# ScalarE, not SyncE, issues half of the weight loads at a change of layer: eight sequences through six layers on one core

## The chip, the cores and the metric

The kernel runs on one core of a Trainium2 chip. The metric is the time of one execution in microseconds (us) on the device. Of three runs of the kernel before, the median is 1677.21 us (1673.2 to 1680.72).

## The reference, cut to what matters

The input `x` is 8 sequences of 256 tokens with 128 channels, in float32. A first attention layer (16 heads of 8) is added to `x`. Then 6 layers follow, each with a windowed attention and a feed-forward part:

```python
for i in range(DEPTH):            # DEPTH = 6
    x = attn_layer(shift_tokens(x), Wqkv[i], q_scale[i], k_scale[i], Wo[i]) + x
    x = ffn_layer(shift_tokens(x), ln_g[i], ln_b[i], W1[i], b1[i], W2[i], b2[i]) + x

def attn_layer(x, Wqkv, qs, ksc, Wo):       # 16 heads of 64, window 32
    q, k, v = split(x @ Wqkv)
    q, k = l2norm(q) * qs, l2norm(k) * ksc  # then a rotary embedding of both
    ...                                     # softmax over this window and the one before
    return out @ Wo
```

## The kernel before, in words

A setup block computes the first attention layer and brings the weights of all six layers into a form of eight *banks* per layer in the device's memory (`weights`, 512 KB a bank): banks 0 and 1 give q, 2 and 3 give k, and 4 to 7 give the product of the value weights with the output projection, `u`. The rest is one pipeline over 48 *units* (`UNITS`), unit n being sequence n % 8 in layer n // 8. Only one layer's banks are resident, in the tile `w_t`.

A step of the pipeline is written out by hand for each engine (the functions `step`), and it mixes stages of up to four units: `after` (the next), `u`, `before` and `last`. The Python loop unrolls all steps, so each engine runs a fixed list of instructions, and semaphores alone tie the engines together. All waits of an instruction are `wait_ge` just ahead of it.

- **TensorE** multiplies the input of a unit, split in a high and a low part, with the banks: `proj(u, t, j)` (L1893, L1898, L1902) for token tile t and bank j, into two banks of PSUM in turn. At the first unit of a layer the first `proj` of each bank waits for that bank's load (`w_in[j]`). It transposes q and k (`transpose_qk`, L1917), makes the scores (`scores`, L1931 and L1939), transposes the probabilities (L1949), multiplies them with `vk` (`values`, L1961) and does the feed-forward part (L1982 to L2031). The banks 0 to 3 of the next unit are used at the end of a step: `proj(after, 0, 0)` to `proj(after, 0, 3)`. For the last unit of a layer their last readers are `proj(u, 1, 0)` to `proj(u, 1, 3)`, in the first half of the same step.
- **ScalarE** squares the q and k products (`square`, L1638), copies transposed q and k into `qT` and `kT` (L1660, L1664), copies `u` into the tile `un` (L1648), copies the transposed probabilities (L1681) and the output `o` (L1691), and computes exponentials and GELU. At the last unit of a layer (`split_layer`) it also makes the high part of the next W1 (`w_hi`, L1763), between `feed_hi` and `copy_qkT(u, 0, 1, 0)`. It issues no DMA.
- **VectorE** makes the sums of the squares, the rotary products and the softmax steps; **GpSimd** the norms and the second half of the rotary embedding.
- **SyncE** issues every DMA. `copy_v(n, t)` rearranges `un` into `vk` by 14 or 16 DMAs (L1255), once `u` of unit n is complete and the values of the unit before are read. `renew(layer, j)` waits until the last unit of the old layer has read bank j and issues the load of 512 KB (`load_weights`, L222). SyncE works through its list in order: between layers it is `copy_v` of unit 6 of the layer, then `renew` of banks 4, 5, 0, 1, 2, 3, 6, 7, then `copy_v` of unit 7.

The semaphore `qk_p` counts the products of banks 0 to 3, eight a unit: `qk_p.at(n, 4 + j)` is reached when token tile 1 has read bank j. `square(u, 1, kind, half)` waits for the same count for j = 2 * kind + half.

Of the kernel before, what the change touches and what calls it, by code (L numbers as in the profile page):

```python
# [33 lines left out]
B = 8  # L34
# [25 lines left out]
UNITS = L * B  # L60
BANKS = 8
QK_BANKS = 4
# [26 lines left out]
def build(nc, x, w_heads, bq_heads, bk_heads, w_v, b_v_rows, w_proj, b_proj_rows, wqk, q_scale_rows, k_scale_rows, wvt, wo,  # L89
          feed_cols, w1, w2, rope, ident, win_mask, win_pick, causal, positions, slope_heads, one_row, weights, out):  # L90
    with ExitStack() as ctx:
# [52 lines left out]
        qk_p = signal("qk_p", 8)  # L144
# [75 lines left out]
        def load_weights(sp, at, j):  # L220
            src = weights[bass.ds(at, 1), :, :].rearrange("o p n -> p (o n)")
            sp.dma_start(w_t[:, j, :, :].rearrange("p k n -> p (k n)").bitcast(F32), src).then_inc(w_in[j].sem, 16)  # L222
# [992 lines left out]
        def index(u):  # L1215

            return u[0] * 2 + u[1]
# [9 lines left out]
        def live(u):  # L1227

            n = index(u)
            return not isinstance(n, int) or 0 <= n < UNITS  # L1230
# [7 lines left out]
        with nc.Block() as block:  # L1238
            @block.sync
            def _(sp):  # L1240
                def copy_v(n, t):


                    value = un_a[t].at(n, 3)
                    sp.wait_ge(av_p.sem, value)
                    sp.wait_ge(un_a[t].sem, value)
                    for w in range(4 * t, 4 * t + 4):
                        for back in (1, 0):
                            if w - back < 0:
                                continue  # L1250
                            tile, k = (w - back) // 4, (w - back) % 4
                            for hp in range(2):
                                lo = 64 * hp + 32 * (1 - back)
                                src = un[32 * k:32 * k + 32, (n % 2) * TT + tile, hp, :]
                                sp.dma_start(vk[lo:lo + 32, w, :, :].rearrange("p a c -> p (a c)"),  # L1255
                                             src).then_inc(vk_in[t].sem, 16)

                def renew(layer, j):
                    qk = j < QK_BANKS
                    at = layer * BANKS + j  # L1260
                    read = qk_p.at(layer * B - 1, QK_BANKS + j) if qk else u_p[0].at(layer * B - 1, j - QK_BANKS)
                    for used in (qk_p,) if qk else u_p:
                        sp.wait_ge(used.sem, read)
                    load_weights(sp, at, j)

                def load_w1(layer):
                    sp.wait_ge(w1l_g.sem, w1l_g.at(layer - 1))
                    sp.dma_start(w1_s[:, :], w1[bass.ds(layer, 1), :, :].rearrange("o p n -> p (o n)")).then_inc(w1_in.sem, 16)

                def load_w2(layer):  # L1270
                    last = w2_p.at(layer * B - 1)
                    sp.wait_ge(w2_p.sem, last)
                    sp.dma_start(w2_s[:, :, :], w2[bass.ds(layer, 1), :, :, :].rearrange("o p k n -> p (o k) n")).then_inc(w2_in.sem, 16)


                sp.wait_ge(zeroed.sem, 1)
                for n in range(2):
                    for t in range(TT):
                        copy_v(n, t)
                for i in range(2):  # L1280
                    sp.wait_ge(qk_stored[i].sem, qk_stored[i].at(L * QK_BANKS // 2 - 1, 15))
                for half in range(2):
                    sp.wait_ge(u_stored[half].sem, u_stored[half].at(L - 1, 15))
                for layer in range(L - 1):
                    for i in range(2, 7):
                        for t in range(TT):
                            copy_v(layer * B + i, t)
                        if i == 4:
                            load_w1(layer + 1)
                    renew(layer + 1, 4)  # L1290
                    renew(layer + 1, 5)
                    renew(layer + 1, 0)
                    renew(layer + 1, 1)
                    renew(layer + 1, 2)
                    renew(layer + 1, 3)
                    renew(layer + 1, 6)
                    renew(layer + 1, 7)
                    copy_v(layer * B + 7, 0)
                    copy_v(layer * B + 7, 1)
                    copy_v(layer * B + 8, 0)  # L1300
                    copy_v(layer * B + 8, 1)
                    copy_v(layer * B + 9, 0)
                    load_w2(layer + 1)
                    copy_v(layer * B + 9, 1)
                for i in range(2, B):
                    for t in range(TT):
                        copy_v(i + (L - 1) * B, t)

                sp.wait_ge(sc_p.sem, sc_p.at(UNITS - 1, 1))
                sp.wait_ge(spilled.sem, 16 * B)  # L1310
                sp.dma_start(x1_again, out.rearrange("b (t p) c -> p (b t) c", p=P)).then_inc(x1_in.sem, 16)
                sp.wait_ge(x1_in.sem, 16)
                for b in range(B):
                    sp.wait_ge(res_d.sem, res_d.at(b))
                    sp.dma_start(out[b, :, :].rearrange("(t p) c -> p t c", p=P), x1_again[:, b * TT:(b + 1) * TT, :]).then_inc(out_done.sem, 16)
                sp.wait_ge(out_done.sem, 16 * B)
# [307 lines left out]
            def _(act):  # L1624
# [6 lines left out]
                def square(u, t, kind, half):  # L1631
# [4 lines left out]
                    if t > 0 or not (isinstance(n, int) and n < 1):  # L1636
                        act.wait_ge(ss_d.sem, ss_d.before(n, 2 * t + kind - 1))
                    S.activation(sq[:, kind, half * 512:(half + 1) * 512], ps[:, PJ + PJ_BANK[t][2 * kind + half], :],  # L1638
                                 ACT.Square).then_inc(sq_a.sem, 1)

                def copy_u(u, t, j):
                    if not live(u):
                        return
                    n = index(u)
                    act.wait_ge(u_p[t].sem, u_p[t].at(n, j))
                    if not (isinstance(n, int) and n < 2):
                        act.wait_ge(vk_in[1].sem, vk_in[1].at(n - 2, vk_in[1].per - 1))
                    S.activation(un[:, (u[1] % 2) * TT + t, j // 2, (j % 2) * HALF:(j % 2 + 1) * HALF],  # L1648
                                 ps[:, PJ + PJ_BANK[t][QK_BANKS + j], :], ACT.Copy).then_inc(un_a[t].sem, 1)
# [131 lines left out]
                def step(m, s):  # L1781
                    after, u, before, last = ((m, s + k) for k in (1, 0, -1, -2))
                    square(u, 0, 0, 1)
                    copy_qkT(before, 1, 0, 1)
                    shift_hi(after)
                    copy_pT(last, 1)
                    square(u, 0, 1, 0)
                    copy_qkT(before, 1, 1, 0)
                    square(u, 0, 1, 1)
                    exps(before, 0)  # L1790
                    root_seed(u, 0)
                    copy_o(last, 1)
                    if index(last) == UNITS - 1:
                        finish_copy(0)
                        finish_copy(1)
                    copy_qkT(before, 1, 1, 1)
                    copy_u(u, 0, 0)
                    residual_hi(last)
                    copy_u(u, 0, 1)
                    copy_u(u, 0, 2)  # L1800
                    copy_u(u, 1, 0)
                    copy_center(last)
                    square_x(last)
                    if index(last) == UNITS - 1:
                        finish_copy(2)
                        finish_copy(3)
                    copy_u(u, 1, 1)
                    square(u, 1, 0, 0)
                    copy_qkT(u, 0, 0, 0)
                    square(u, 1, 0, 1)  # L1810
                    copy_qkT(u, 0, 0, 1)
                    copy_pT(before, 0)
                    square(u, 1, 1, 0)
                    square(u, 1, 1, 1)
                    if index(last) == UNITS - 1:
                        finish_copy(4)
                        finish_copy(5)
                    feed_scale(last)
                    if index(last) == UNITS - 1:
                        finish_copy(6)  # L1820
                    feed_cols(before)
                    feed_hi(last)
                    copy_qkT(u, 0, 1, 0)
                    exps(before, 1)
                    root_seed(u, 1)
                    copy_qkT(u, 0, 1, 1)
                    copy_o(before, 0)
                    gelu(last, 0)
                    copy_u(u, 1, 2)
                    copy_u(u, 1, 3)  # L1830
                    gelu(last, 1)
                    copy_u(u, 0, 3)
                    copy_qkT(u, 1, 0, 0)
                    square(after, 0, 0, 0)
                    gelu(last, 2)
# [375 lines left out]
```

## Time and profile before

| | us |
|---|---|
| median of three runs | 1677.21 |
| the profiled execution, its time | 1680.03 |
| the profiled execution, its span | 1678.2 |
| TensorE, matmuls busy | 1620.7 (97%) |
| VectorE busy | 1478.2 (88%) |
| GpSimd busy | 1331.9 (79%) |
| ScalarE busy | 1328.8 (79%) |
| mean granted clock of TensorE | 0.992 of full |

The times of single instructions come from the profiled execution. PE stands for TensorE's matmuls, PEld for its weight loads, DVE for VectorE, ACT for ScalarE, POOL for GpSimd, SPq for SyncE's queue of DMA issues. The duration of an issue is the time of the issuing queue, not that of the transfer; the time to landing counts from the start of the issue until the data are there. A name such as `w_t<-weights_dram` is output<-input. The brackets at the end of a row of a timeline give the idle time of the engine ahead of the instruction and what ended it; "issue" stands there where the profile shows no releaser.

### The profile page before, as it was taken

To read this page: it belongs to the slowest core of one execution; us is meant where nothing else is said; L and a number is where in the kernel's file an instruction comes from. 1 tells how busy PE (TensorE), PEld (TensorE's weight loads), DVE (VectorE), ACT (ScalarE), POOL (GpSimd) and SP (SyncE) were. 2 spreads that over 40 slices of the span, in tenths; PEclk is the share of its full clock that TensorE was granted. 3 is DMA by queue.
4 is the path that set the end of the run, shared out by engine and by line. 5 is a ranking of instruction groups with operands and counts; after the bars stand their busy time and mean duration, and the time that the engine had idled before them with its cause. 6 is when DMAs were issued, how large, how long until landed. Compare 5 with 4: busy or idle time off the path is not lost.

```text
span 1678.2 us, 70646 instructions
## 1 busy us (share of the span) xinstructions
PE 1620.7 (97%) x29222; PEld 1410.5 (84%) x29222; DVE 1478.2 (88%) x2314; ACT 1328.8 (79%) x2789; POOL 1331.9 (79%) x1798
## 2 busy tenths in 40 slices
PE   7999869999999999999999999999999999999997
PEld 5777647888889889898988989898898988889886
DVE  6887749999899999899999999999999998999984
ACT  6888746878778788888878888787888887888874
POOL 7777568888788888888888788888888888888870
PEclk9999989999999999999999999999999999999999
DMA  3588517565865656857566765658566667656654
GB/s 125 176 295 323 199 26 162 119 147 133 231 146 128 155 128 155 228 128 164 119 159 167 194 146 134 149 128 244 124 154 137 143 150 207 156 128 148 139 131 111
DMA packets 101407, 265.78 MB, mean 158 GB/s; under 512 B 26720, under 2 KB 34912, under 8 KB 101088
## 3 DMA queue, kind: packets, MB, share of 16 engines
q1 hardware_dynamic: 101088, 261.26, 61.6%
q8 instruction: 232, 3.80, 1.0%
q14 instruction: 87, 0.71, 0.1%
HBM read 45.15 MB, written 27.26 MB: 43 GB/s over the span
## 4 chain that ended last, share of the span: by engine, by line
PE 74%; POOL 4%; SPq 3%; issue 2%; ACT 2%; DVE 1%; DMA 1%; POOLq 0%; ACTq 0%; DVEq 0%
PE ps L1893 17%; PE ps L1902 13%; PE ps L1961 9%; PE ps L1917 9%; PE ps L1939 7%; PE ps L1949 4%; PE ps L2031 3%; SPq L1255 3%; PE ps L2018 2%; PE ps L2020 2%; PE ps L2019 2%; PE ps L1931 2%; POOL rot L1339 1%; POOL rot L1397 1%; PE ps L1992 1%
## 5 line engine op out<-in xcount | busy, mean ns | idle before, releaser
L1339 POOL TENSOR_TENSOR rot<-rot 128x512 f32<-128x512 f32 x380 | 491.6, 1309 | 45.6 <-DVE rot L1474 45.6
L1474 DVE TENSOR_TENSOR rot<-ps,rope_l 128x1024 f32<-128x1024 f32 x380 | 462.8, 1219 | 27.4 <-ACT sq L1638 15.0
L1397 POOL TENSOR_TENSOR rot<-rot,rnorm 128x1024 f32<-128x1024 f32 x190 | 361.9, 1905 | 17.7 <-POOL rnorm L1367 0.4
L1648 ACT ACTIVATE un<-ps 128x512 f32<-128x512 f32 x384 | 229.6, 598 | 102.3 <-PE ps L1893 41.7
L1893 PE MATMUL ps<-w_t,xs_hi 128*128 128x512 f32 x880 | 298.0, 419 | 5.6 <-issue 3.8
L1902 PE MATMUL ps<-w_t,xs_hi 128*128 128x256 f32 x1284 | 262.9, 297 | 14.9 <-PEq L374 11.1
L1638 ACT ACTIVATE sq<-ps 128x512 f32<-128x512 f32 x380 | 227.8, 599 | 51.7 <-PE ps L1893 29.1
L1460 DVE TENSOR_REDUCE ssum<-sq 128x16 f32<-128x1024 f32 x190 | 229.9, 1210 | 13.7 <-ACT sq L1638 13.7
L1917 PE MATMUL ps<-ident_s,rot 128*128 128x128 f32 x1536 | 234.3, 275 | 6.0 <-ACT kT L1664 4.1
L1902 PEld LDWEIGHTS ps<-w_t,xs_hi 128*128 128x128 f32 x1284 | 196.3, 190 | 25.3 <-issue 20.4
L1917 PEld LDWEIGHTS ps<-ident_s,rot 128*128 128x128 f32 x1536 | 179.5, 140 | 40.9 <-issue 20.6
L1961 PE MATMUL ps<-vk,pT 128*32 128x128 f32 (+1 forms) x6624 | 189.6, 267 | 0.6 <-ACT pT L1681 0.6
L1902 PE MATMUL ps<-w_t,xs_lo 128*128 128x256 f32 x642 | 180.4, 281 | 0.0
L1961 PEld LDWEIGHTS ps<-vk,pT 128*32 128x32 f32 x6624 | 163.8, 110 | 16.6 <-issue 15.7
L1893 PEld LDWEIGHTS ps<-w_t,xs_hi 128*128 128x128 f32 x880 | 138.4, 189 | 35.3 <-ACT un L1648 8.4
L1893 PE MATMUL ps<-w_t,xs_lo 128*128 128x512 f32 x389 | 154.4, 397 | 0.0
L1939 PEld LDWEIGHTS ps<-kT,qT 64*32 64x32 f32 x12288 | 146.0, 105 | 7.6 <-issue 1.3
L1939 PE MATMUL ps<-kT,qT 64*32 64x64 f32 x12288 | 149.3, 225 | 0.4 <-issue 0.2
L1902 PEld LDWEIGHTS ps<-w_t,xs_lo 128*128 128x128 f32 x642 | 121.3, 189 | 0.0
L1518 DVE TENSOR_TENSOR prob<-ps,linv 128x1024 f32<-128x1024 f32 x96 | 117.6, 1225 | 3.1
L1485 DVE TENSOR_REDUCE smax<-ps 128x16 f32<-128x1024 f32 x96 | 116.5, 1213 | 3.1 <-PE ps L1939 3.1
L1502 DVE TENSOR_REDUCE lsum<-ps 128x16 f32<-128x1024 f32 x96 | 116.6, 1215 | 2.7 <-ACT ps L1672 2.7
(158 smaller groups left out, 3565.1 us busy)
## 6 DMA issues: line engine op xcount, KB each, us to landing
vk<-un SPq DMA_DIRECT2D x1440, 128.0 KB
w_t<-weights_dram SPq DMA_DIRECT2D x48, 512.0 KB, 6.9
weights_dram<-rot SPq DMA_DIRECT2D x12, 1024.0 KB, 5.1
weights_dram<-sq SPq DMA_DIRECT2D x24, 512.0 KB, 3.7
raw<-wqk_dram SPq DMA_DIRECT2D x24, 256.0 KB, 4.2
wvt_s<-wvt_dram SPq DMA_DIRECT2D x12, 256.0 KB, 5.3
wo_s<-wo_dram SPq DMA_DIRECT2D x12, 256.0 KB, 6.4
w_s<-w_dram SPq DMA_DIRECT2D x6, 341.0 KB, 4.3
```

The costliest lines, as they stand in the source:

```text
L1339: last = G.tensor_tensor(cos[:, :, s, :], cos[:, :, s, :], sin[:, :, 1 - s, :], ALU.add)
L1397: G.tensor_tensor(v, v, rnorm[:, t, kind * H:(kind + 1) * H, None].broadcast_to([P, H, D]), ALU.mult).then_inc(nrm_g.sem, 1)
L1460: V.tensor_reduce(ssum[:, t, kind * H:(kind + 1) * H], sq[:, kind, :].rearrange("p (h e) -> p h e", h=H), AX_X, ALU.add).then_inc(ss_d.sem, 1)
L1474: V.tensor_tensor(dst, src[:, None, :, :].broadcast_to([P, 2, H // 2, D]), tab[:, :, None, :].broadcast_to([P, 2, H // 2, D]), ALU.mult).t ...
L1518: V.tensor_tensor(pairs, tile_scores(t).rearrange("p (hp a) k -> p hp a k", hp=2), inv, ALU.mult).then_inc(pn_d.sem, 1)
L1638: S.activation(sq[:, kind, half * 512:(half + 1) * 512], ps[:, PJ + PJ_BANK[t][2 * kind + half], :], ACT.Square).then_inc(sq_a.sem, 1)
L1648: S.activation(un[:, (u[1] % 2) * TT + t, j // 2, (j % 2) * HALF:(j % 2 + 1) * HALF], ps[:, PJ + PJ_BANK[t][QK_BANKS + j], :], ACT.Copy).t ...
L1893: last = M.matmul(bank, v, w_t[:, j, w, :], start=i == 0, stop=i == 2)
L1902: last = M.matmul(bank[:, cols], v, w_t[:, j, w, cols], start=i == 0, stop=i == 2)
L1917: last = M.transpose(ps[:, TP, a * P:(a + 1) * P], rot[:, kind, 0, c * P:(c + 1) * P], ident_s[:, :])
L1939: last = M.matmul(out_s, qT[rows, par, a, 32 * w:32 * w + 32], kT[rows, a, 32 * w:32 * w + 64], start=False, stop=a == PAIRS - 1)
L1961: last = M.matmul(ps[32 * k:32 * k + 32, SO[t], cols], pT[:, a, 32 * k:32 * k + 32], vk[:, 4 * t + k, a, cols], start=a == 0, stop=a == PA ...
```

## The change

ScalarE gets a function `renew_qk`, which issues the load of one of banks 0 to 3 in the step of a layer's last unit, each behind the square of the same bank's product of token tile 1. SyncE keeps banks 4, 5, 6 and 7 in their order.

```diff
                     renew(layer + 1, 4)
                     renew(layer + 1, 5)
-                    renew(layer + 1, 0)
-                    renew(layer + 1, 1)
-                    renew(layer + 1, 2)
-                    renew(layer + 1, 3)
                     renew(layer + 1, 6)
                     renew(layer + 1, 7)
...
+                def renew_qk(u, j):
+                    if not live(u) or index(u) % B != B - 1 or index(u) == UNITS - 1:
+                        return
+                    n = index(u)
+                    act.wait_ge(qk_p.sem, qk_p.at(n, QK_BANKS + j))
+                    load_weights(act, (n // B + 1) * BANKS + j, j)
...
                     square(u, 1, 0, 0)
+                    renew_qk(u, 0)
                     copy_qkT(u, 0, 0, 0)
                     square(u, 1, 0, 1)
+                    renew_qk(u, 1)
                     copy_qkT(u, 0, 0, 1)
                     copy_pT(before, 0)
                     square(u, 1, 1, 0)
+                    renew_qk(u, 2)
                     square(u, 1, 1, 1)
+                    renew_qk(u, 3)
```

## Rows read from the trace of the kernel before

**Rows 1.** The page's busy times, with share of the span and instructions.
```profile
PE 1620.7 (97%) x29222; PEld 1410.5 (84%) x29222; DVE 1478.2 (88%) x2314; ACT 1328.8 (79%) x2789; POOL 1331.9 (79%) x1798
```

**Rows 2.** The chain that ended last, at the fifth change: start, duration, engine, line.
```profile
1383.95 1.48 SPq L222
1386.43 8.48 DMA w_t<-weights_dram
```

**Rows 3.** SyncE's issues at the changes (durations ns, minimum/median/maximum); timeline at the fifth.
```profile
1369.92 13.93 SPq L1255 DMA_DIRECT2D vk<-un  x18
...
L1255 SPq DMA_DIRECT2D vk<-un x13: 590/592/1734, 1374.5 to 1383.3; - x13
...
L222 SPq DMA_DIRECT2D w_t<-weights_dram x1: 422/422/422, 444.3 to 444.3; - x1
...
DMA to landing us min/median/max: 6.3/6.3/6.3
...
L222 SPq DMA_DIRECT2D w_t<-weights_dram x8: 319/435/1741, 677.5 to 686.3; - x8
...
L222 SPq DMA_DIRECT2D w_t<-weights_dram x8: 319/436/1750, 1149.0 to 1157.0; - x8
...
L222 SPq DMA_DIRECT2D w_t<-weights_dram x40: 319/424/1750, 443.2 to 1391.2; - x40
...
DMA to landing us min/median/max: 3.4/7.3/11.5
```

**Rows 4.** Timeline of ScalarE at the fifth change: start, duration, line, operation.
```profile
1377.38 0.60 ACT L1638 ACTIVATE sq<-ps 128x512 f32<-128x512 f32 x1
...
1378.97 0.60 ACT L1638 ACTIVATE sq<-ps 128x512 f32<-128x512 f32 x1 [0.50 <-PE ps L1893]
...
1380.28 1.03 ACT L1681 ACTIVATE pT<-ps 128x1024 f32<-128x1024 f32 x1 [0.22 <-PE ps L1949]
1381.20 1.29 ACT L1638 ACTIVATE sq<-ps 128x512 f32<-128x512 f32 x2
1382.39 0.59 ACT L1750 ACTIVATE xg<-xg,cur 128x256 f32<-128x256 f32 x1
```

**Rows 5.** Windows: length, busy PE, PEld, DVE, ACT, POOL; clock, DMA share, GB/s.
```profile
475.30:490.65 15.35, 15.35 (x307) 14.34 (x306) 14.96 (x18) 13.38 (x23) 12.38 (x20) 1.00 0.42 95
...
441.14:461.50 20.36, 17.38 (x303) 15.79 (x303) 15.50 (x18) 14.37 (x24) 13.57 (x21) 0.92 0.93 299
...
679.11:695.99 16.88, 15.72 (x304) 14.23 (x303) 14.98 (x18) 14.21 (x24) 13.92 (x21) 1.00 0.96 324
913.83:931.95 18.12, 15.82 (x304) 14.32 (x303) 15.15 (x18) 14.20 (x24) 13.61 (x21) 1.00 0.90 307
1149.79:1166.66 16.87, 15.73 (x303) 14.23 (x303) 14.97 (x18) 14.22 (x24) 13.88 (x21) 1.00 0.98 327
1384.18:1402.78 18.60, 16.07 (x303) 14.33 (x303) 15.32 (x18) 14.20 (x24) 13.58 (x21) 1.00 0.95 309
...
450.00:458.00 8.00, 7.28 (x47) 7.05 (x48) 4.78 (x6) 4.57 (x9) 3.80 (x4) 0.79 1.02 337
```

**Rows 6.** Timeline of TensorE at the first, third and fifth change.
```profile
441.68 0.63 PE L1917 MATMUL ps<-ident_s,rot 128*128 128x128 f32 x4 [0.54 <-ACT kT L1664]
...
444.08 0.41 PE L1931 MATMUL ps<-wmask,wpick 64*32 64x512 bf16 x8 [0.38 <-ACT o L1691]
...
450.72 0.71 PE L1893 MATMUL ps<-w_t,xs_hi 128*128 128x512 f32 x2 [2.06 <-issue]
...
922.72 0.71 PE L1893 MATMUL ps<-w_t,xs_hi 128*128 128x512 f32 x2 [1.38 <-issue]
...
1392.04 0.71 PE L1893 MATMUL ps<-w_t,xs_hi 128*128 128x512 f32 x2 [0.35 <-issue]
...
1394.95 0.51 PE L1902 MATMUL ps<-w_t,xs_hi 128*128 128x256 f32 x2 [1.26 <-DMA w_t<-weights_dram]
...
1398.13 0.48 PE L1902 MATMUL ps<-w_t,xs_hi 128*128 128x256 f32 x2
```

## The prediction

> **What bounds it.** I read the busy times first, then the chain that ended last, then the windows of the layer changes, then single engines inside them. TensorE's matmuls cover 97% of the span [rows 1], so a change that moves no arithmetic can give back only stretches in which TensorE stands still. There are five layer changes. At the last of them the chain leaves TensorE: it runs over SyncE's weight issue (L222) and then over one weight load that lands 8.48 us after its issue [rows 2]. What to see: SyncE is busy with `vk` copies from 1369.92 on [rows 3], and only at 1383.95 does it come to the first weight load. Bank 0's last reader of the old layer was done by then: ScalarE's square of it started at 1377.38 [rows 4].
>
> How much is at stake is in the windows of half a step, from the end of `values(before, 0)` to the end of `values(before, 1)` [rows 5]. An ordinary one takes 15.35 us; the five at a change take 20.36, 16.88, 18.12, 16.87 and 18.60. The excess is 5.01 + 1.53 + 2.77 + 1.52 + 3.25 = 14.1 us. TensorE's own rows say where it stands still [rows 6]. Two waits, 0.54 us before `transpose_qk` (released by ScalarE's copy into `kT`) and about 0.4 before `scores` (released by ScalarE's copy of `o`), belong to ScalarE: at this step it also makes `w_hi`. They make, with their surroundings, the 1.5 us that the second and fourth change show with no other gap; the change leaves that as it is. On top come 2.06 us at the first change, 1.38 at the third, and 0.35 + 1.26 at the fifth, all before the first products with new weights. Only the last is labelled as a wait for the load; but at the first change bank 0 was issued at 444.3 and landed 6.3 us later, at 450.6 [rows 3], and TensorE went on at 450.72. I read the others, labelled "issue", the same way. After the 2.06 us of idleness the granted clock fell to the lower level, 1.2 GHz, for part of the next 8 us: 0.79 of full over them [rows 5]. What the first half step has beyond 1.5 and 2.06 is 1.4 us, and that is its price.
>
> **What goes.** 14.1 less 5 × 1.52 leaves 6.5 us that come from late weights (3.5 + 1.25 + 1.75; nothing at the second and fourth). Behind the square of 1377.38 bank 0 can be issued, where SyncE issued it third in its row, near 1386: some 8 us earlier. Bank 3 can go behind the squares at 1381.20 to 1382.49, some 5 us earlier. TensorE wants bank 0 at 1391.7 (the end of the gap less its 0.35), so bank 0 has 14.3 us, and the longest landing of the forty is 11.5 [rows 3]. The loads now meet the copies: 18 of these, 128 KB each, went out in 13.93 us [rows 3], which is 170 GB/s, while 8 us at the first change moved 337 GB/s on average [rows 5]. If the loads got only the difference, bank 0's 512 KB would take 3 us and all four 12.6 us, to 1390 from 1377.4; bank 3 is wanted last, at 1398.1 [rows 6]. So the stalls go whole. The lower clock of the first change should go with the idle stretch before it. Sum: -6.5 us.
>
> The `vk` copies of unit 6 that share the engines are wanted by `values(6, 1)`, which ends at 1402.78 [rows 5], over 15 us after the last of them is issued; landing some us later costs nothing. SyncE loses four issues of 0.42 us and nobody waits for them: it then stands at `renew(…, 7)`, which waits for `proj(u, 0, 7)` as before, and `copy_v(7, …)` starts at the same point. Banks 4 to 7 move up by at most 1.7 us and were not late. The new waits on ScalarE (`qk_p`) are those of the square just ahead, so they hold nothing up. TensorE, VectorE and GpSimd get no instruction.
>
> **What comes.** ScalarE gets four DMA issues per change, 20 in all. No row shows an issue on ScalarE. The nearest is the same instruction on SyncE: 0.42 us in the middle, with one each of 1.74, 1.75 and 1.48 at the second, fourth and fifth change [rows 2, 3]. From below the price is nothing: records on ScalarE overlap by 0.1 us already (1380.28 + 1.03 against 1381.20), and its sequencer may issue while the engine works on a square of 0.60 us [rows 4]. From above it is all of it, 4 × 0.42 = 1.7 us, less the 0.50 and 0.22 us in which ScalarE stands idle behind the first two [rows 4], so 1.0 us per change. What is behind matters: after the second pair of squares ScalarE runs back to back up to the `kT` copy for which TensorE already waits 0.54 us, so each tenth exposed there is a tenth on the path. Each of those squares, though, starts when TensorE's product ends, and has 0.6 us of its own, more than an issue takes. I take 0.1 us per change, nearer to nothing, 0.5 in all. A long issue is not covered by a square: 20 × 3/40 = 1.5 of them, 1.3 us over the ordinary each, 2.0 us. In sum -6.5 + 0.5 + 2.0 = **-4.0 us**. The profiled execution took 1680.0 us, 2.8 above the median of the three; it would come to 1676.0, and the median to **1673.2 us**.
>
> **A rule that speaks against it.** SyncE issues copies without a pause while ScalarE would issue its four [rows 3]. The Trainium skill, "Perfetto Trace Analysis", section "DMA Instruction — HWDGE (DVE, Sync)", says that descriptor generation is a block shared by two issuing sequencers, and that the profiled duration includes the wait for its lock. No run shown has a second issuer, so the trace can't say. By that rule the sum is the one of the rivals B and C below, whose prices come from the rows.
>
> **Rivals.** B, the issues are partly exposed because ScalarE waits for SyncE's issue in progress: half of 0.59, the time of one copy issue, makes each 0.42 + 0.3 = 0.72 us; behind the last two squares 0.1 to 0.4 each stays over 0.60, 0.2 to 0.9 per change, or the 1.0 of the upper bound. With the long ones: -6.5 + 1 to 5 + 2 = -3.5 to +0.5, about 1676 us. For it: SyncE's back-to-back burst. Against: it needs a coupling that no row shows.
> C, **slower**: the issue blocks ScalarE outright and waits a whole copy issue too. Per change 4 × (0.42 + 0.59) - 0.72 = 3.3 us, directly before the `kT` copy, 16.6 in five, and the long ones 2; -6.5 + 18.6 = +12.1, 1689 us. It decides as soon as more than 1.3 us per change are exposed, since only 6.5 us are to be had; over 3.0 us, the long ones with them, it is slower by more than 0.5%. Against: the squares start from TensorE's ends, so not all of ScalarE's time is on the path.
> D, **faster by more**: the executions that were not profiled lose more to late weights (they spread over 7.5 us), or ScalarE's own waits at the change also shrink because less piles up behind the late weights. All 14.1 us would give 1663. Against: those waits lie ahead of the first use of new weights.
> E, **it does not bring the loads forward in effect**: sharing with the copies, they land as late as before. Then nothing goes and 2.5 us come: 1680. Against: 8 us of head start.
>
> **Chances.** My forecast 0.50, B 0.26, C 0.12, D 0.07, E 0.05. A measurement of this kernel can tell about 0.5% (8.4 us) from no change; the forecast, B and E lie inside. So faster 0.07, same 0.81, slower 0.12. The range runs from 1668, the forecast without any cost (1670.7) and some of D, to 1683, beyond B and E and into C's lesser forms; it leaves out D's full size and C's.
>
> **What would show it.** Right: 20 weight issues on ScalarE's queue, 28 left on SyncE's; no gap before the first three projections of the new layer; half steps at the change of 16.9 to 17.1 us, all five alike; the 0.54 us before `transpose_qk` grown by 0.1 or so; no lower clock at the first change. Wrong: that gap at 1 us or more and the second and fourth half steps longer than 16.9 by the same (B, C); issues on ScalarE longer than 0.7 us (the shared block); gaps that stay before the new weights (E). The second and fourth changes are the cleanest test, since they have a cost and no gain.

## The result, and the profile after

The changed kernel takes 1684.7 us (median of 6 runs, 1683.79 to 1687.77) against 1676.53 us for the kernel before (median of 6, with three further runs): a ratio of 1.0049, 95% interval 1.0034 to 1.0064. It is slower by 8.2 us, where 4 us less were forecast, and outside the range. The profiled execution took 1685.4 us, with a span of 1683.6 us, 5.4 above that of the kernel before.

First ScalarE's side. The view is the timeline of ScalarE at the fifth change in the kernel after; ACTq is its queue of DMA issues.

```profile
1381.30 0.60 ACT L1634 ACTIVATE sq<-ps 128x512 f32<-128x512 f32 x1
1381.31 0.33 ACTq L222 DMA_DIRECT2D w_t<-weights_dram  x1
1381.79 0.59 ACT L1663 ACTIVATE qT<-ps 128x512 f32<-128x512 f32 x1
1382.88 0.60 ACT L1634 ACTIVATE sq<-ps 128x512 f32<-128x512 f32 x1 [0.50 <-PE ps L1900]
1382.89 0.33 ACTq L222 DMA_DIRECT2D w_t<-weights_dram  x1
1383.38 0.59 ACT L1663 ACTIVATE qT<-ps 128x512 f32<-128x512 f32 x1
1384.19 1.03 ACT L1684 ACTIVATE pT<-ps 128x1024 f32<-128x1024 f32 x1 [0.23 <-PE ps L1956]
1385.11 0.33 ACTq L222 DMA_DIRECT2D w_t<-weights_dram  x1
1385.12 1.28 ACT L1634 ACTIVATE sq<-ps 128x512 f32<-128x512 f32 x2
1385.81 0.39 ACTq L222 DMA_DIRECT2D w_t<-weights_dram  x1
```

Each issue runs under its square, and the 0.50 and 0.23 us of idleness are those of [rows 4]. So ScalarE pays next to nothing here. Over all five changes, the view of the line that issues the loads says nearly the same, beside SyncE's back-to-back copies: 0.33 us in the middle, 18 of the 20 at most 0.39. The longest, 0.80 us at the second change, left ScalarE idle for 0.31 us behind it.

```profile
L222 ACTq DMA_DIRECT2D w_t<-weights_dram x20: 326/330/796, 436.4 to 1385.8; - x20
L222 SPq DMA_DIRECT2D w_t<-weights_dram x20: 319/352/537, 442.3 to 1399.2; - x20
```

The waits for the new weights are gone too. But the same half steps as in [rows 5], from the end of `values(before, 0)` to the end of `values(before, 1)`, are not shorter:

```profile
443.21:463.22 20.01, 17.05 (x303) 15.54 (x303) 15.34 (x18) 14.25 (x25) 13.72 (x21) 0.91 0.89 257
681.24:699.52 18.28, 15.70 (x304) 14.38 (x303) 15.24 (x18) 14.54 (x25) 14.29 (x21) 1.00 0.96 286
917.10:935.37 18.27, 15.70 (x303) 14.39 (x303) 15.34 (x18) 14.12 (x24) 13.64 (x21) 1.00 0.97 288
1152.84:1170.75 17.91, 15.75 (x304) 14.41 (x303) 15.25 (x18) 14.12 (x24) 13.90 (x21) 1.00 1.01 302
1388.08:1408.55 20.47, 17.09 (x304) 15.58 (x303) 15.35 (x18) 14.14 (x24) 13.61 (x21) 0.92 0.94 266
```

They hold 18.2 us over 15.35 each, where those of before held 14.1. The timeline of TensorE shows what is new, at the second to the fifth change (at the first it is the same instruction, 1.93 us). Its first row is the wait before `transpose_qk` at the second change, 0.54 us before:

```profile
682.21 0.63 PE L1924 MATMUL ps<-ident_s,rot 128*128 128x128 f32 x4 [0.96 <-ACT kT L1667]
...
687.09 0.71 PE L1946 MATMUL ps<-kT,qT 64*32 64x64 f32 x47 [1.01 <-issue]
...
922.92 0.71 PE L1946 MATMUL ps<-kT,qT 64*32 64x64 f32 x47 [1.66 <-issue]
...
1158.28 0.71 PE L1946 MATMUL ps<-kT,qT 64*32 64x64 f32 x47 [1.01 <-issue]
...
1394.72 0.88 PE L1946 MATMUL ps<-kT,qT 64*32 64x64 f32 x47 [2.45 <-issue]
```

TensorE stops in the middle of `scores(u, 0)`, behind the 81st of its 128 products (x47 are left), at all five changes. No product in there waits for a semaphore: `scores` waits ahead of its first product alone. The five gaps make 8.1 us. Behind the two longest, 1.93 and 2.45 us, the granted clock is again at its lower level for a while (0.91 and 0.92 over the half steps).

A stop without a wait, always at one instruction, suggests that the instructions themselves are late. The profile has a queue for them, q8: 232 packets and 3.80 MB in all, so 16.4 KB each. TensorE's matmuls and weight loads are 58444 of the 70646 instructions, which makes 252 to a packet if this queue is TensorE's. (A second one, q14, has 87 packets with 0.70 MB.) The DMA view of a narrow stretch shows whether one of these packets ran in it. In the kernel before, the third one of the first change's step runs 13.1 us after the step's start at 427.54:

```profile
DMA packets 102, 0.27 MB, mean 111 GB/s; under 512 B 40, under 2 KB 40, under 8 KB 101
## 3 DMA queue, kind: packets, MB, share of 16 engines
q1 hardware_dynamic: 101, 0.25, 48.2%
q8 instruction: 1, 0.02, 3.9%
```

That is the stretch 440.6 to 443.0. In the kernel after the step starts at 429.39, so the same packet is due near 442.5. From 442.5 to 446.7 there is none, only loads (q10 is ScalarE's queue, q1 SyncE's):

```profile
DMA packets 346, 1.11 MB, mean 264 GB/s; under 512 B 75, under 2 KB 75, under 8 KB 346
## 3 DMA queue, kind: packets, MB, share of 16 engines
q10 hardware_dynamic: 167, 0.61, 56.6%
q1 hardware_dynamic: 179, 0.50, 46.3%
```

and it comes from 446.7 on:

```profile
DMA packets 126, 0.41 MB, mean 270 GB/s; under 512 B 30, under 2 KB 30, under 8 KB 125
## 3 DMA queue, kind: packets, MB, share of 16 engines
q10 hardware_dynamic: 62, 0.22, 55.4%
q1 hardware_dynamic: 63, 0.17, 41.1%
q8 instruction: 1, 0.02, 5.0%
```

This packet starts at 446.81 and ends at 448.00; TensorE, dry since 447.50, goes on at 449.43. At the five changes the packet starts 16.5 to 17.4 us into the step instead of 13.0 to 13.6, and each time TensorE goes on 1.4 to 1.6 us after its end. This suggests theory T1: **the early loads hold up TensorE's instruction fetch on the shared DMA engines.** The rival, T2, is that issuing from ScalarE, or its having a DMA queue of its own, costs the time.

### The profile page after: what moved, and what is told of

The parts are those of the page before. It is cut to its first block, busy times and chain, and to the rows that moved or that the text cites. A ratio compares the mean times of both kernels' runs of the same rounds, so it can differ in the third digit from the quotient of the medians.

```text
span 1683.6 us, 70646 instructions
## 1 busy us (share of the span) xinstructions
PE 1623.2 (96%) x29222; PEld 1413.9 (84%) x29222; DVE 1478.9 (88%) x2314; ACT 1327.5 (79%) x2789; POOL 1331.9 (79%) x1798
## 4 chain that ended last, share of the span: by engine, by line
PE 75%; POOL 3%; SPq 2%; issue 2%; ACT 2%; DVE 1%; DMA 0%; POOLq 0%; ACTq 0%; DVEq 0%
PE ps L1900 17%; PE ps L1909 13%; PE ps L1968 9%; PE ps L1924 9%; PE ps L1946 7%; PE ps L1956 4%; PE ps L2038 4%; SPq L1255 2%; PE ps L2025 2%; PE ps L2026 2%; PE ps L2027 2%; PE ps L1938 2%; POOL rot L1335 1%; PE ps L1999 1%; PE ps L1905 1%
## 5 line engine op out<-in xcount | busy, mean ns | idle before, releaser
L1909 PE MATMUL ps<-w_t,xs_hi 128*128 128x256 f32 x1284 | 263.0, 297 | 13.6 <-PEq L374 11.0
L1634 ACT ACTIVATE sq<-ps 128x512 f32<-128x512 f32 x380 | 227.6, 599 | 44.7 <-PE ps L1900 24.2
L1968 PEld LDWEIGHTS ps<-vk,pT 128*32 128x32 f32 x6624 | 163.9, 110 | 16.6 <-issue 15.6
```

Source lines behind the costliest of these rows:

```text
L1909: last = M.matmul(bank[:, cols], v, w_t[:, j, w, cols], start=i == 0, stop=i == 2)
L1968: last = M.matmul(ps[32 * k:32 * k + 32, SO[t], cols], pT[:, a, 32 * k:32 * k + 32], vk[:, 4 * t + k, a, cols], start=a == 0, stop=a == PA ...
```

## The experiments

All were made of one of the two kernels; ratios are to the kernel before on the same chip. The starts of the fetch packet are in us after the step's start, from the records of queue q8, over the five changes. The gaps are those of the profiled execution, in us: behind the 81st product of `scores(u, 0)`, and behind the 27th product of the scores one half step on, where the next but one packet is needed. The ratios rest on 10 to 12 executions each, in e5 and e9 on 4, in e6 and after on 6.

| run | early loads ahead of the fetch | fetch packet starts | gaps, 81st product | gaps, 27th, next half step | ratio (95%) |
|---|---|---|---|---|---|
| before | none | 13.0 to 13.6 | 0 | 0 | 1 |
| after | banks 0 to 3, ScalarE | 16.5 to 17.4 | 8.1 | 0 | 1.0049 (1.0034 to 1.0064) |
| e1 | four of 4 KB, ScalarE | 13.0 to 14.0 | 0 | 0.6 | 1.0001 (0.9988 to 1.0014) |
| e2 | banks 0 to 3, SyncE | 15.0 to 16.4 | 1.5 | 3.2 | 1.0038 (1.0026 to 1.0050) |
| e3 | none at all | 13.2 to 13.4 | 0 | 0 | 0.9979 (0.9967 to 0.9990) |
| e4 | none, banks 0 to 3 first | 13.3 to 13.7 | 0 | 1.3 | 0.9988 (0.9979 to 0.9998) |
| e5 | halves of banks 0 to 3 | 15.5 to 17.9 | 4.5 | 0 | 1.0041 (1.0025 to 1.0057) |
| e6 | none, ScalarE 16 to 17 us in | 13.2 to 13.8 | 0 | 0 | 1.0103 (1.0078 to 1.0129) |
| e7 | banks 0 and 1 | 14.8 to 16.0 | 1.0 | 1.5 | 0.9999 (0.9990 to 1.0008) |
| e8 | banks 0 to 3, few copies | 14.9 to 15.8 | 0 | 0 | 0.9988 (0.9979 to 0.9998) |
| e9 | banks 2 and 3 | 16.2 to 17.4 | 7.3 | 0 | 1.0051 (1.0035 to 1.0066) |
| e11 | e4 again | 13.0 to 15.1 | 0 | 2.7 | 0.9995 (0.9983 to 1.0007) |

**e1, ScalarE's issues without the bytes.** SyncE loads everything as before; ScalarE issues four DMAs of 4 KB at the changed kernel's places.

```diff
-                    load_weights(act, (n // B + 1) * BANKS + j, j)
+                    act.dma_start(tiny[:, n // B, j, :], weights[(n // B + 1) * BANKS + j, :, 0:8]).then_inc(tiny_in[j].sem, 16)
```

> All eight weight loads stay with SyncE as before the change; ScalarE issues four extra DMAs of 4 KB each at the places where the changed kernel issues banks 0 to 3. Theory T1 (the early loads hold up TensorE's instruction fetch on the shared DMA engines): the issues cost ScalarE nothing that shows, no gap inside the scores, the fetch of about 13 us into the step stays at 13, time within 2 us of the kernel before (ratio 0.999 to 1.001). Rival T2 (issuing from ScalarE, or its own DMA queue, costs the time): most of the 8 us stays, ratio 1.003 to 1.005.

Ratio 1.0001, and no stop behind the 81st product. Issuing from ScalarE and a queue of its own cost nothing by themselves, so T2 falls in this form. (Whether the bytes cost more in a queue of their own is another question; see e2.) The line's view shows issues as long as in the kernel after:

```profile
L1648 ACTq DMA_DIRECT2D tiny<-weights_dram x20: 326/327/371, 436.1 to 1378.0; - x20
```

**e2, the bytes without ScalarE.** SyncE issues banks 0 to 3 among the copies of unit 6, token tile 1: behind the 4th, 6th, 8th and 9th. The four old calls are taken out.

```diff
+AMONG = {4: (0,), 6: (1,), 8: (2,), 9: (3,)}
...
                                 sp.dma_start(vk[lo:lo + 32, w, :, :]...).then_inc(vk_in[t].sem, 16)
+                                done += 1
+                                for j in between.get(done, ()):
+                                    renew(n // B + 1, j)
```

> SyncE issues banks 0 to 3 itself, between the vk copies of unit 6, at the moments at which the changed kernel issues them on ScalarE; ScalarE issues nothing. T1: the same gap of 1 to 2.5 us inside the scores at each change, the fetch comes 3 to 4 us late, ratio 1.003 to 1.006. T2: as the kernel before or faster, ratio 0.996 to 1.000, no gap inside the scores.

Ratio 1.0038, 1683.0 us in the median: most of the loss, with ScalarE left alone. The fetch is 2 to 3 us late. The profiled execution was among the fastest of its ten (1678.2 us), and in it only the first change has the gap at length (two more have 0.1 and 0.2 us). It is the one in TensorE's timeline:

```profile
447.57 0.71 PE L1940 MATMUL ps<-kT,qT 64*32 64x64 f32 x47 [1.20 <-issue]
```

A fetch that starts by 15.5 us costs at most 0.2 us there; the one that started at 16.4 cost 1.20. The limit agrees with TensorE's own pace: it is dry some 17.9 us into the step, and goes on 1.5 us after a packet of 1.2 us.

Four of the five changes have another gap one half step on, behind the 27th product, 0.35 to 1.17 us; it comes again in e4. And one thing of T2 stays open. With the same loads at the same moments, the fetch started at 15.0 to 16.4 us from SyncE's queue and at 16.5 to 17.4 from ScalarE's. In the profiled executions the gaps behind the 81st product made 1.5 against 8.1 us; the medians, 1683.0 and 1684.7, lie closer. Loads in a second queue may hold the fetch up more; no run separates that.

**e3, the floor.** Banks 0 to 3 are loaded for layer 0 alone, and the waits for them with n > 0 are left out; layers 1 to 5 compute q and k with the weights of layer 0.

```diff
-                    if t == PJ_FIRST[j] and n % B == 0:
+                    if t == PJ_FIRST[j] and n % B == 0 and (n == 0 or j >= QK_BANKS):
```

> Banks 0 to 3 are loaded for layer 0 only; the loads at the five changes are left out with their waits, so layers 1 to 5 compute q and k with the weights of layer 0. Both theories: no gap before the first products of the new layer, half steps of 16.9 us or less at all five changes, 6 to 8 us below the kernel before (ratio about 0.996). T1 adds: the fetches at 13 and 17.5 us into the step come at their ordinary places.

Ratio 0.9979: without these loads the kernel gains 3.5 us (1.7 to 5.5 by the interval), less than the 6 to 8 expected. The five half steps hold 6.9 us over 15.35 each: this is ScalarE's share, as read before. So late weights cost the kernel before some 3.5 us in a usual execution, if the missing loads save nothing else; in its profiled one, at 1680.0, it was 14.1 - 6.9 = 7.2. That this varies between executions shows in e1: SyncE loads all banks there in the old order, and in its profiled execution (1675.2 us) the five half steps take 16.6 to 16.9 us, with no wait for weights. From this floor the kernel after is 11.3 us away in its profile: 8.1 in the gaps, 0.6 in longer waits for `kT`, the rest mostly in the slower stretches behind the two longest gaps.

**e4 and e11, another order on SyncE.** Only the list changes; banks 0 to 3 go ahead of 4 and 5.

```diff
-                    renew(layer + 1, 4)
-                    renew(layer + 1, 5)
                     renew(layer + 1, 0)
                     renew(layer + 1, 1)
                     renew(layer + 1, 2)
                     renew(layer + 1, 3)
+                    renew(layer + 1, 4)
+                    renew(layer + 1, 5)
```

> All loads stay with SyncE at the old time, but banks 0 to 3 go ahead of banks 4 and 5. T1: bank 0 lands 3.5 us after its issue instead of 6.3, near 19 us into the step and ahead of its use at 21.1; the gaps of 2.06, 1.38 and 1.6 us go and the fetch at 13 us stays on time: 3 to 6.5 us faster than the kernel before (ratio 0.996 to 0.998). Rival (the loads as a whole, in whatever order, hold up the later fetch at 17.5 us): the gap moves elsewhere, ratio 0.999 to 1.001.

> The reordered list on SyncE once more, for a tighter interval: ratio 0.998 to 0.9995, half steps of 16.6 to 16.9 us at the changes, as without any loads of banks 0 to 3.

In both profiles all five half steps take 16.6 to 16.9 us, as in e3: no wait for weights, and no gap behind the 81st product. But the time moves less than I expected, 0.9988 and 0.9995, which is 0.8 to 2.0 us (by the intervals up to 3.5, or nothing). The next half step says why it falls short of e3. In e4 it has gaps of 0.12 and 1.21 us at the first and third change, in e11 gaps of 1.85, 0.72 and 0.12 us at the last three. TensorE's timeline at the third change, of e4 and then of e11:

```profile
933.48 1.21 PE L1939 MATMUL ps<-kT,qT 64*32 64x64 f32 x101 [1.21 <-issue]
```

```profile
932.70 1.29 PE L1939 MATMUL ps<-kT,qT 64*32 64x64 f32 x101 [1.85 <-issue]
```

It is the same kind of stop, behind the 27th product: the packet ahead of it starts at 29.1 to 31.8 us into the step, against 28.2 to 29.5 in e3, and TensorE goes on 1.4 to 1.6 us after its end. SyncE's own last load, bank 7, lands at 28.2 to 31.8 us, in e3 at 24.2 to 25.6. In the kernel before the packet starts at 28.7 to 32.9 us and there is no gap; it is late (30.8 and more) only at the three changes at which TensorE, by its waits for weights, is late too. So with these waits gone, a late packet shows: this is what the rival in e4's expectation said, at another packet than it named. That half step of e11, where ordinary ones take 13.8 us, took 17.33, with the lower clock in part of it:

```profile
928.39:945.72 17.33, 15.48 (x264) 13.12 (x265) 12.52 (x16) 10.68 (x22) 11.97 (x15) 0.90 0.81 201
```

By its ratios this order is the best of the versions that compute everything, though not clearly better than the kernel before, and it beats the changed kernel by more than 7 us.

**e5, half the bytes.** ScalarE loads the first half (256 KB) of each bank at the changed kernel's places, SyncE the second at the old place.

```diff
-                    load_weights(act, (n // B + 1) * BANKS + j, j)
+                    load_half(act, (n // B + 1) * BANKS + j, j, 0)
...
-                    load_weights(sp, at, j)
+                    load_half(sp, at, j, 1) if qk else load_weights(sp, at, j)
```

> ScalarE issues, at the changed kernel's places, only the first half (256 KB) of banks 0 to 3; SyncE issues the second halves at the old place. T1 (bytes of early loads on the shared DMA engines delay TensorE's instruction fetch): the fetch at 13 us into the step starts at 14.5 to 15.5 instead of 16.2 to 17.2, which is just in time, so gaps inside the scores vanish or shrink below 0.5 us; ratio 0.998 to 1.001. T2 (issues from ScalarE or the order of events on ScalarE cost): as the changed kernel, 1.004 to 1.005, since the number and the place of its issues are the same.

A miss: 1.0041 was expected of T2, not of T1. The packet starts at 15.5 to 17.9, and the gaps are where T1 has them, up to 2.51 us:

```profile
682.82 0.87 PE L1954 MATMUL ps<-kT,qT 64*32 64x64 f32 x47 [2.51 <-issue]
```

So the fetch is late, but halving the bytes does not halve the delay. Rows of 2 KB in place of 4 KB keep the number of packets; and banks 2 and 3 are still issued just ahead of the fetch. Of the first, e1 says something: ScalarE's queue q10 moved as many packets there as in the kernel after, and with next to no bytes the fetch was on time. So their number alone does not hold it up. From the pages of e1 and of the kernel after:

```profile
q10 hardware_dynamic: 2880, 0.08, 0.1%
q10 hardware_dynamic: 2880, 10.49, 2.3%
```

The next two runs take up the second.

**e7 and e9, two banks early.** e7 leaves banks 0 and 1 with ScalarE (7 and 8.5 us into the step), e9 banks 2 and 3 (10.8 and 11.4); SyncE has the other two behind 4 and 5.

```diff
-                    renew_qk(u, 2)
...
-                    renew_qk(u, 3)
```

(e7; e9 takes out the calls for 0 and 1.)

> ScalarE issues banks 0 and 1 in full at the changed kernel's places, SyncE banks 4, 5, 2, 3, 6, 7. T1: 1 MB instead of 2 MB ahead of the fetch; it starts near 14 to 15.5 us, no or little idleness in the scores, and no wait for banks 0 and 1: ratio 0.997 to 1.001. T2: about half of the loss, 1.002 to 1.003.

> Like the run with two early loads, but it is banks 2 and 3 that ScalarE issues at the changed kernel's places (10.8 and 11.4 us into the step), and SyncE has banks 4, 5, 0, 1, 6, 7. If the amount ahead of the fetch decides, it is as with banks 0 and 1: fetch at 14.6 to 15.8 us, ratio 0.999 to 1.001. If it is what is still outstanding when the fetch is asked for at 13 us, the two late ones do most of the harm: fetch at 15.5 to 17 us, gaps of 0.5 to 2 us inside the scores, ratio 1.002 to 1.005 (banks 0 and 1 wait again as in the kernel before, too).

The same 1 MB, and two results: 0.9999 and 1.0051. With banks 2 and 3 the packet starts at 16.2 to 17.4, as late as with all four, and the gap is back:

```profile
448.69 0.71 PE L1946 MATMUL ps<-kT,qT 64*32 64x64 f32 x47 [1.42 <-issue]
...
1157.80 0.71 PE L1946 MATMUL ps<-kT,qT 64*32 64x64 f32 x47 [1.83 <-issue]
```

So what was issued before is not what counts. What is still outstanding at about 13 us, when the fetch is due, fits: in e7 bank 0 had landed by 12.5 us and bank 1 landed at 15.5 to 16.3, in e9 both were under way, to 14.9 to 15.5 and 17.4 to 18.8. This is read from two runs and not shown further.

**e8, the changed kernel with small copies.** The 16 copies of unit 6, token tile 1, move 64 B a row instead of 4 KB, so that tile's values come from stale data; the issues stay.

```diff
+                    size = 16 if n % B == 6 and t == 1 and n // B < L - 1 else PAIRS * C
...
-                                src = un[32 * k:32 * k + 32, (n % 2) * TT + tile, hp, :]
+                                src = un[32 * k:32 * k + 32, (n % 2) * TT + tile, hp, 0:size]
```

> The changed kernel, but the 16 vk copies of unit 6 of each layer but the last, token tile 1, move 64 B a row instead of 4 KB (the values of that tile are then those of stale data); the number of issues is the same. T1 in the form that the loads and the copies together crowd the fetch out: the fetch moves back to 13 to 14.5 us and the gap inside the scores goes, ratio 0.996 to 0.999. If the loads alone do it, the fetch stays at 15.5 to 17 and the ratio at 1.003 to 1.005.

The packet is still 2 us late (14.9 to 15.8), between what I expected of either form, but in time, and the ratio is 0.9988, the floor of e3 within the intervals. There is no gap one half step on either. The loads alone delay the fetch by 2 us; with the copies beside them it is 3 to 4, and that is over the limit.

**e6, ScalarE late.** All four issues stand behind `copy_o(before, 0)`, when the fetch is through.

```diff
                     copy_o(before, 0)
+                    renew_qk(u, 0)
+                    renew_qk(u, 1)
+                    renew_qk(u, 2)
+                    renew_qk(u, 3)
```

> ScalarE issues banks 0 to 3 in full, but all four behind copy_o(before, 0), some 16 us into the step, when the fetch at 13 us is done; SyncE keeps banks 4 to 7. T1: no gap inside the scores, the fetch at 13 us on time, bank 0 lands by 21 us: ratio 0.997 to 0.999, like the reordered list on SyncE or 1 us better. T2: above 1.002.

The fetch is on time and the scores have no gap, as T1 says, but the time is a miss: 0.997 to 0.999 was expected, and it is the slowest of the runs in the table at 1.0103. Two things that I had not counted show. Four issues in a row are no longer under anything; ScalarE's timeline:

```profile
448.35 0.44 ACTq L222 DMA_DIRECT2D w_t<-weights_dram  x1
448.49 0.27 ACT L1694 ACTIVATE o<-ps 128x128 f32<-128x128 f32 x1
448.83 0.98 ACTq L222 DMA_DIRECT2D w_t<-weights_dram  x2
449.84 1.28 ACT L1775 ACT_TABLE_LOAD   x1 [1.08 <-issue]
```

The table load, and with it GELU and the feed-forward products behind, comes about a microsecond later; TensorE waits 0.7 to 1.3 us for `hid`. And the loads share the engines with SyncE's banks 4 to 6 in a second queue, so that they land late, and TensorE waits for them again:

```profile
PE ps L2025 <- DVE hid L1551: 6.4, 8, 1.3
PE ps L1909 <- DMA w_t<-weights_dram: 6.2, 4, 2.2
```

(the waits of TensorE, in total, number, longest). At three changes bank 3 landed only 30 us into the step, and three further waits, 2.6 us in sum and labelled "issue", end as bank 0 lands. Together the waits at the changes make 13.4 of the 17.5 us by which the five half steps are longer than in e3; the rest was not followed up.

**e10 and e12, the stream shifted.** Forty transposes on TensorE ahead of the pipeline, 80 instructions, in the changed kernel and in the kernel before.

```diff
                 pe.sem_inc(av_p.sem, av_p.start)
+                for _ in range(40):
+                    M.transpose(ps[:, TP, 0:P], ident_s[:, :], ident_s[:, :])
```

> The changed kernel with 40 more transposes on TensorE ahead of the pipeline (80 instructions, some 3 us once). If the gap inside the scores is TensorE running out of fetched instructions, its place is tied to the instruction stream: it moves 40 pairs earlier at all five changes, from behind the 81st to behind the 41st of the 128 score products. If it is anything tied to the data or to another engine, it stays behind the 81st.

> The kernel before with the same 40 transposes ahead of the pipeline. If the gaps in the ordinary steps of the padded changed kernel come from where the instruction stream is cut for its fetches, they are here too: about 45 to 50 us over the kernel before, gaps behind the 114th or 115th score product in every second step. If they need the loads on ScalarE, the time is within 5 us of the kernel before.

The gap moved at one change only, and the shift did far more than I expected. The padded changed kernel took 1730.7 us and the padded kernel before 1737.1, one run each, 53 and 59 us over the kernel before; both end the values of their first unit only 1 to 5 us later than without the padding, so the transposes themselves are not it. At the changes of e10 four of the five gaps are gone and the fifth stands behind the 41st product, 40 earlier:

```profile
1429.68 0.63 PE L1948 MATMUL ps<-kT,qT 64*32 64x64 f32 x41
...
1431.15 1.06 PE L1948 MATMUL ps<-kT,qT 64*32 64x64 f32 x85 [0.84 <-issue]
```

In place of them there are 33 gaps in the scores of ordinary steps, behind the 105th and the 114th or 115th product, with or without the change (e12 has as good as the same). The waits of TensorE in e10, then in e12:

```profile
PE ps L1948 <- issue: 41.3, 34, 2.3
```

```profile
PE ps L1941 <- issue: 42.0, 31, 2.0
```

In e12 a packet starts at 528.36 and lasts 1.49 us, and TensorE, dry behind the 115th product, goes on 1.4 us after its end, at 531.24:

```profile
528.34 1.34 PE L1941 MATMUL ps<-kT,qT 64*32 64x64 f32 x115
...
531.24 0.34 PE L1941 MATMUL ps<-kT,qT 64*32 64x64 f32 x13 [1.56 <-issue]
```

The place of a stop moves with the count of instructions, nothing else was changed, and each stop ends 1.0 to 1.6 us behind a packet. That shows that TensorE ran out of instructions. At e10's changes the packet started at 14.3 to 15.6, in e12 without early loads at 12.0 to 12.3: still 2 to 3 us late, but only the latest gave a stop. With the fetches at another place in the stream, the loads do not meet them as they did.

## Why the prediction was wrong

- **What bounds it** held. The waits for late weights were real and went in the changed kernel; e3 and e4 remove them too. ScalarE's share stayed in the floor of e3 (6.9 us in all, I had 7.6).
- **What goes** was too large: 6.5 us from one profiled execution, which lay 2.8 us above the median. e3 measures 3.5. I said that the executions differ, but did not cut the term. Nor is a wait that goes all gained: e4 and e11, without those waits, gave back 2.0 and 0.8 us.
- **What comes** was right for ScalarE. I took 0.1 us per change; the waits before `transpose_qk` grew by 0.13, 0.42, 0, 0 and 0.02. Of the long issues, priced at 2.0 us, one came, of 0.80 us, and it is the change whose wait grew by 0.42; by my own sign (over 0.7 us) it could be the shared block, but it is one of 20. The Trainium skill's rule of that block ("Perfetto Trace Analysis", section "DMA Instruction — HWDGE (DVE, Sync)") stood behind rivals B and C; the 0.33 us of a usual issue beside back-to-back copies speak against it mattering here.
- **The step that failed** is "the loads now meet the copies". I asked of that meeting only when the loads and the copies land. (Even there my sum was too short, without harm: all four banks landed 22.1 to 24.2 us into the step, where it had 19.4.) The third user of the DMA engines is TensorE's instruction stream, a line in the page's list of queues, and it has no semaphore by which it would show up as a wait. It was forecast at nothing. In its place the runs showed five stops of 8.1 us in sum and the slower stretches behind two of them: at the five changes the kernel after stands 11.3 us over the floor in its profile, nearly all of it from the late fetch and what follows. Less the 3.5 us gained (a difference of medians) that is 7.8, beside the 8.2 measured.
- **The slower rival, C,** had the right sign and the wrong mechanism; e1 rules it out. The test that I had named, the second and fourth half steps, did its work: they grew by 1.4 and 1.0 us with ScalarE's part in them only 0.4 and 0 (the wait before `transpose_qk`).
- Open: why a packet, once due, waits 3 to 4 us though its queue is its own. e5, e7, e8 and e9 say only that outstanding loads and copies do it, late ones most. The number of packets alone does not (e1); how the delay goes with the bytes, and what a second queue adds (e2), was not settled.

## What to carry to other kernels

Before a transfer is moved to an earlier place, look at what else runs on the DMA engines there, the engines' own instruction fetches included: an unrolled kernel that keeps TensorE at small products (here 256 instructions in 1.5 us) lives on them, and their delay shows as idleness with the releaser "issue" in a place without a wait. Order the loads by first use before moving them to another engine; here that took two moved lines and removed the waits for weights, though a later fetch took a part of the gain. Look at the half steps behind the change as well as at the one it aims at. Here a DMA issue was as good as free on ScalarE where it stood under a longer instruction, and four in a row left it idle for 1.08 us.

## What the runs showed of the hardware that was not expected

TensorE's instruction stream comes in packets of 16.4 KB (3.80 MB in 232). The late ones at the changes of the kernel after lasted 1.2 us each, and TensorE went on 1.4 to 1.6 us after their end. The Trainium skill, "Runtime: NRT & Kernel Launch", section "Instruction fetch mechanics", says that instructions are refilled in 16 KB blocks through a DMA queue of the sequencer, with which the packets agree, and that the cost of crossing a block is mostly hidden. Here it was hidden in the kernel before, but not with loads outstanding beside it (1.0 to 2.5 us a stop), and not in the one other alignment tried: 80 instructions more at the start came with 53 and 59 us, one execution each.

In the kernel after, the stops of 1.93 and 2.45 us were each followed by 3.4 us at the lower level of TensorE's clock, 1.2 GHz, as was the one of 2.06 us in the kernel before; those of 1.0 and 1.66 us were not. The length of the stop does not decide it alone: in e9 one of 1.37 us was followed by the lower level and those of 1.42 and 1.66 were not, and in e10 one of 2.32 us was not. ScalarE's issue of a DMA ran beside its own square, and took 0.33 us in the middle whether it moved 4 KB or 512 KB; in e6, four in a row beside SyncE's loads, it took 0.44.
